# Expert results added onto the kept rows in DRAM by accumulating scatters, in place of a stage that gathers each token's pair of results

## The reference, cut to what matters

```
x = x + gnn(layernorm(x), ...)                       # three attention layers
xf = layernorm(x)
router_logits = einsum('th,eh->te', xf, Wr)
topk_vals, topk_idx = top_k(router_logits, 2)
routing_weights = softmax(topk_vals)
h = gelu(einsum('th,efh->etf', xf, Wi) + bi)
expert_out = einsum('etf,ehf->eth', h, Wo) + bo
out = einsum('tk,tkh->th', routing_weights, the two chosen rows of expert_out)
x = x + out
```

## Time and profile before

| | us |
|---|---|
| median of 3 runs (3463.12 to 3468.98) | 3465.05 |
| the profiled execution | 3468.89 |
| its span, first to last instruction | 3467.1 |
| PE busy | 2769.7 |
| DVE busy | 2306.3 |
| POOL busy | 1486.6 |
| ACT busy | 869.1 |

### The profile page before, as it was taken

The page is one execution under the profiler, slowest core; times in us unless marked ns, Lnnn a source line. Parts: engine busy times, 40 slices in busy tenths (PEclk is TensorE's granted clock), DMA queues, the critical chain, the costliest instruction groups (busy, mean ns, idle before and its releaser), DMA issues.

```text
span 3467.1 us, 58417 instructions
## 1 busy us (share of the span) xinstructions
PE 2769.7 (80%) x14425; PEld 1927.4 (56%) x14426; DVE 2306.3 (67%) x4402; ACT 869.1 (25%) x1640; POOL 1486.6 (43%) x1569
## 2 busy tenths in 40 slices
PE   0797999999889799999979989999994544999910
PEld 0685555555578555555548855555553444677700
DVE  8647999999877699999987746666664444122233
ACT  0221222222244222222234423433431111111100
POOL 1002676767400466676730067777760000211133
PEclk9997999999989899999989989999995555899955
DMA  2334999999744699999964479999976651333366
GB/s 104 100 110 143 312 308 313 312 311 308 239 148 156 214 308 307 311 316 312 307 205 156 150 271 325 331 327 329 329 273 221 221 194 47 110 131 132 123 229 235
DMA packets 225304, 804.36 MB, mean 232 GB/s; under 512 B 35255, under 2 KB 74576, under 8 KB 225252
## 3 DMA queue, kind: packets, MB, share of 16 engines
q0 software_dynamic: 117456, 582.67, 47.6%
q1 hardware_dynamic: 86654, 162.71, 15.9%
q10 hardware_dynamic: 21142, 58.39, 4.3%
HBM read 692.95 MB, written 111.09 MB: 232 GB/s over the span
## 4 chain that ended last, share of the span: by engine, by line
PE 35%; DVE 20%; DMA 17%; POOL 10%; issue 10%; ACT 5%; ACTq 2%; DVEq 1%; SPq 1%; POOLq 0%
PE PS L824 15%; DMA arena<-table,src_k 11%; POOL arena L514 10%; PE PS L932 4%; PE PS L756 4%; PE PS L921 3%; DMA arena<-table 3%; DMA arena<-expert_out,chosen 2%; PE PS L758 2%; DVE parts L1220 2%; DVE arena L1203 2%; PE PS L905 1%; DVE arena L1084 1%; DVE arena L1100 1%; DVE arena L1099 1%
## 5 line engine op out<-in xcount | busy, mean ns | idle before, releaser
L514 POOL DMA_INDIRECT arena<-table,src_k x1260 | 1296.7, 1029 | 522.2 <-PE PS L824 296.5
L824 PE MATMUL PS<-arena,S 128*128 128x396 f32 (+1 forms) x2688 | 992.7, 508 | 9.7 <-DVE arena L1203 9.7
L1203 DVE TENSOR_TENSOR arena<-arena,PS 128x768 f32<-128x768 f32 x840 | 766.1, 944 | 0.9 <-ACT arena L650 0.9
L824 PEld LDWEIGHTS PS<-arena,S 128*128 128x128 f32 x2688 | 470.7, 190 | 240.5 <-issue 28.3
L824 PE MATMUL PS<-parts,S 128*128 128x384 f32 (+2 forms) x1344 | 326.8, 365 | 123.0 <-DVE parts L1220 87.9
L824 PE MATMUL PS<-arena,S_weighted 128*128 128x384 f32 x1008 | 385.2, 511 | 22.6 <-issue 12.5
L801 PEld LDWEIGHTS PS<-erp,ST_b 128*128 128x128 bf16 x3780 | 220.0, 97 | 321.2 <-issue 228.0
L756 PE MATMUL PS<-W_split,S 128*128 128x512 f32 x900 | 358.9, 416 | 27.7 <-DVE xT_rest L1123 27.2
L470 POOL DMA_DIRECT2D table<-arena x75 | 40.7, 543 | 659.9 <-ACT arena L570 635.8
L824 PEld LDWEIGHTS PS<-parts,S 128*128 128x128 f32 x1344 | 220.5, 190 | 138.3 <-issue 137.6
L801 PE MATMUL PS<-erp,ST_b 128*128 x3780 | 254.0, 172 | 14.9 <-DVE ST_b L1169 11.5
(11 more groups left out here) (222 smaller groups left out, 3652.9 us busy)
## 6 DMA issues: line engine op xcount, KB each, us to landing
local_b<-local SPq DMA_DIRECT2D x252, 160.0 KB, 5.6
mixed<-sums ACTq DMA_DIRECT2D x75, 384.0 KB, 6.4
arena<-mixed SPq DMA_DIRECT2D x75, 384.0 KB, 3.8
arena<-table SPq DMA_DIRECT2D x75, 384.0 KB, 5.1
expert_out<-arena SPq DMA_DIRECT2D x56, 384.0 KB, 2.4
arena<-table,src_k POOLq DMA_INDIRECT x1260, 5.3
table<-arena POOLq DMA_DIRECT2D x50, 390.0 KB, 3.4
arena<-in_x SPq DMA_DIRECT2D x48, 384.0 KB, 4.1
```

What stands on the lines that cost most here:

```text
L514: nc.gpsimd.indirect_dma_start(edge_rows(l)[:, k % U, 0:D + HEADS[l]], None, table[l][:, :], bass.IndirectOffsetOnAxis(src_k[:, k:k + 1].b ...
L824: o = nc.tensor.matmul(flat[:, bass.ds(odd * 1024 + 512 * c, n)], onehot, row[:, c * HALF:c * HALF + n], start=False, stop=True, skip_grou ...
L1203: nc.vector.tensor_tensor(z, z, a, ALU.mult).then_inc(s_msg, 1)
```

## The change

Each expert result is multiplied by its gate when DVE copies it out of PSUM, and POOL adds it with an indirect accumulating DMA straight onto the token's row of `x2_kept`. When all 56 slots are added, SP and ACT copy `x2_kept` to the output, from DRAM to DRAM, in two large pieces and one small one. The pair stage, `expert_out`, `chosen` and the two gather helpers of the pair stage are gone.

For this, the gate of each place and slot is found as the token is: two more products of one-hots and gates (`at_gate`) on DVE and 50 more matmuls on PE. Places without a token (gate 0) are aimed at 128 spare rows behind the kept ones, which SP fills with zeros at the start. Two adds may touch the same token, so POOL waits for the landing of add n-1 before it issues add n.

POOL's stages are no longer in a loop: they are written out, with the gather of slot n+2 ahead of the add of slot n. `token_of` is indexed directly.

```
+            sp.wait_ge(s_const, 6)
+            sp.dma_start(x2_kept[NPAD:NPAD + P, :], zeros[:, 0:D]).then_inc(s_spare, 16)
...
+            for q in range(2):
+                sp.wait_ge(s_added[q], 16 * (NS // 2))
+            sp.dma_start(out_rows(0, 8), kept_rows(0, 8)).then_inc(s_out_sp, 16)
+            sp.dma_start(out[N // COPY * COPY:N, :], x2_kept[N // COPY * COPY:N, :]).then_inc(s_out_sp, 16)
+            sp.wait_ge(s_out_sp, 32)
...
+            def gather_tokens(n):
+                if n >= 2:
+                    pool.wait_ge(s_xgTp, n - 1)
+                nc.gpsimd.indirect_dma_start(in0(n % 2), None, normed[:, :], bass.IndirectOffsetOnAxis(
+                    token_of[:, n:n + 1].bitcast(U32), 0)).then_inc(s_xg[n % 2], 16)
+
+            def add_to_tokens(n):
+                pool.wait_ge(s_y, n + 3)
+                if n:
+                    pool.wait_ge(s_added[(n + 1) % 2], 16 * ((n + 1) // 2))
                 pool.sem_inc(s_tick)
+                nc.gpsimd.indirect_dma_start(x2_kept[:, :], bass.IndirectOffsetOnAxis(
+                    target_of[:, n:n + 1].bitcast(U32), 0), zr(n % 2, D), None, compute_op=ALU.add).then_inc(s_added[n % 2], 16)
...
             pool.wait_ge(s_routed, 1)
-            sweep_nodes(pool, [(gather_tokens, 0)], count=NS)
-            for q in range(2):
-                pool.wait_ge(s_y_st[q], 16 * (NS // 2 + 1))
-            sweep_nodes(pool, [(gather_pairs, 0)])
+            for n in range(2):
+                gather_tokens(n)
+            pool.wait_ge(s_spare, 16)
+            pool.wait_ge(s_gates, 1)
+            for n in range(NS):
+                if n + 2 < NS:
+                    gather_tokens(n + 2)
+                add_to_tokens(n)
...
+            act.dma_start(out_rows(8, 15), kept_rows(8, 15)).then_inc(s_out_act, 16)
+            act.wait_ge(s_out_act, 16)
...
             o.then_inc(s_tokens_p, 1)
+            pe.wait_ge(s_gated, 2)
+            for m in range(NB * TOP):
+                o = nc.tensor.matmul(PS[:, 7, 0:NS], at_place()[:, m, :], at_gate(m % TOP)[:, m // TOP, :],
+                                     start=(m == 0), stop=(m == NB * TOP - 1))
+            o.then_inc(s_gates_p, 1)
             pe.wait_ge(s_routed, 1)
+            pe.wait_ge(s_gates, 1)
...
+            for j, g in enumerate((g0, g1)):
+                link(tt(at_gate(j), at_slot().rearrange("p (b j) s -> p b j s", j=TOP)[:, :, j, :],
+                   g.unsqueeze(2).broadcast_to([P, NB, NS]), ALU.mult))
+            dve.sem_inc(s_gated, 2)
...
+            row, spare = routing("row"), routing("spare")
+            nc.vector.tensor_copy(token_of[:, :], PS[:, 6, 0:NS]).then_inc(s_routed, 1)
+            link(ts(spare, zeros[:, 0:NS], own[:, 0:1], float(NPAD), ALU.add, ALU.add))
+            link(tt(row, PS[:, 6, 0:NS], spare, ALU.subtract))
+            dve.wait_ge(s_gates_p, 1)
             for q in range(2):
                 link(nc.vector.memset(hT(q)[FH:FH + 1, :], 1.0))
-            nc.vector.tensor_copy(token_of[:, :], PS[:, 6, 0:NS]).then_inc(s_routed, 1)
+            link(nc.vector.tensor_copy(gate_of[:, :], PS[:, 7, 0:NS]))
+            link(nc.vector.scalar_tensor_tensor(out=row, in0=gate_of[:, :], scalar=0.0, in1=row, op0=ALU.is_gt, op1=ALU.mult))
+            tt(target_of[:, :], row, spare, ALU.add).then_inc(s_gates, 1)
+            dve.wait_ge(s_gates, 1)
 
             def copy_y(b):
                 dve.wait_ge(s_down, b.n + 1)
-                dve.wait_ge(s_y_st[b.q], 16 * b.turn + 16)
-                nc.vector.tensor_copy(zr(b.q, D).rearrange("p (c d) -> p c d", c=2),
-                                      PS[:, 4 + 2 * b.q:6 + 2 * b.q, 0:HALF]).then_inc(s_y, 1)
+                if b.reuse:
+                    dve.wait_ge(s_added[b.q], 16 * b.turn)
+                nc.vector.tensor_scalar(zr(b.q, D).rearrange("p (c d) -> p c d", c=2),
+                                        PS[:, 4 + 2 * b.q:6 + 2 * b.q, 0:HALF], gate_of[:, bass.ds(b.n, 1)], None,
+                                        ALU.mult).then_inc(s_y, 1)
...
-            sweep_nodes(dve, [(result, 0)], dc, 2)
```

More of the change, by code:

```diff
@@ L41 @@
 NS = (TOP * N + EX * (P - 1)) // P
+COPY = 13
 NO_NODE = -1.0
@@ L101, in gnn_ffn @@
         normed = nc.dram_tensor("normed", (NPAD, D), F32, kind="Internal").ap()
-        x2_kept = nc.dram_tensor("x2_kept", (NPAD, D), F32, kind="Internal").ap()
-        expert_out = nc.dram_tensor("expert_out", (NS * P, D), F32, kind="Internal").ap()
+        x2_kept = nc.dram_tensor("x2_kept", (NPAD + P, D), F32, kind="Internal").ap()
         local = nc.dram_tensor("local", (V, P), BF16, kind="Internal").ap()
@@ L130, in gnn_ffn @@
         token_of = sb("token_of", [P, NS], I32)
+        target_of = sb("target_of", [P, NS], I32)
+        gate_of = sb("gate_of", [P, NS])
         place_of = sb("place_of", [P, NB, TOP], I32)
         expert_at = sb("expert_at", [1, NS // 2, 4], I32)
-        chosen = sb("chosen", [P, 4], I32)
         ident = sb("ident", [P, P])
@@ L201, in gnn_ffn @@
         s_onehots = sem("s_onehots"); s_tokens_p = sem("s_tokens_p"); s_routed = sem("s_routed")
-        s_xg = [sem("s_xg0"), sem("s_xg1")]; s_chosen = sem("s_chosen"); s_xgTp = sem("s_xgTp"); s_xgT = sem("s_xgT")
+        s_xg = [sem("s_xg0"), sem("s_xg1")]; s_xgTp = sem("s_xgTp"); s_xgT = sem("s_xgT")
         s_up = sem("s_up"); s_gelu = sem("s_gelu"); s_hTp = sem("s_hTp"); s_hT = sem("s_hT"); s_down = sem("s_down")
-        s_y = sem("s_y"); s_y_st = [sem("s_y_st0"), sem("s_y_st1")]
-        s_ab = [sem("s_ab0"), sem("s_ab1")]; s_x2in = [sem("s_x2in0"), sem("s_x2in1")]; s_or = sem("s_or")
-        s_or_st = [sem("s_or_st0"), sem("s_or_st1")]
+        s_y = sem("s_y"); s_added = [sem("s_added0"), sem("s_added1")]
+        s_spare = sem("s_spare"); s_gated = sem("s_gated"); s_gates_p = sem("s_gates_p"); s_gates = sem("s_gates")
+        s_out_sp = sem("s_out_sp"); s_out_act = sem("s_out_act")
         s_dve = sem("s_dve"); s_acts = sem("s_acts"); s_pool = sem("s_pool"); s_den = sem("s_den"); s_tick_act = sem("s_tick_act"); s_tick_dve = sem("s_tick_dve")
@@ L303, in gnn_ffn @@
         sizes = dict.fromkeys(("lg", "pairs", "t", "one0", "one1", "upto", "other"), NB * EX)
-        sizes |= dict.fromkeys(("best", "v0", "v1", "d", "e", "g0", "g1", "token", "real"), NB)
-        sizes |= dict.fromkeys(("place", "slot"), NB * TOP)
+        sizes |= dict.fromkeys(("best", "v0", "v1", "d", "e", "token", "real"), NB)
+        sizes |= dict.fromkeys(("place", "slot", "gates"), NB * TOP)
         sizes |= dict.fromkeys(("rising", "slots", "last_slot", "swap", "slots_i"), EX)
-        sizes["expert"] = NS
+        sizes |= dict.fromkeys(("expert", "row", "spare"), NS)
         def routing(name):
@@ L317, in at_place, with at_gate @@
         def at_place():
-            return arena[:, 0:NB * TOP * P].rearrange("p (m n) -> p m n", n=P)
+            return arena[:, 2 * D:2 * D + NB * TOP * P].rearrange("p (m n) -> p m n", n=P)
         def at_slot():
-            return arena[:, NB * TOP * P:NB * TOP * (P + NS)].rearrange("p (m n) -> p m n", n=NS)
+            return arena[:, 2 * D + NB * TOP * P:2 * D + NB * TOP * (P + NS)].rearrange("p (m n) -> p m n", n=NS)
+        def at_gate(j):
+            base = ST[:, :, :, :].rearrange("p a b c -> p (a b c)") if j else W_rest[:, F + sum(sizes.values()):]
+            return base[:, 0:NB * NS].rearrange("p (m n) -> p m n", n=NS)
         def ended_at():
-            return arena[0:1, NB * TOP * (P + NS):NB * TOP * (P + NS) + NS * EX].rearrange("o (s e) -> o s e", e=EX)
+            return arena[0:1, 2 * D + NB * TOP * (P + NS):2 * D + NB * TOP * (P + NS) + NS * EX].rearrange("o (s e) -> o s e", e=EX)
         def xT_lead(q):
@@ L342, in erm_flat, with out_rows, kept_rows @@
             return erm[:, :, :].rearrange("p b h -> p (b h)")[:, 0:NB * 2 * HEADS[l]]
+        def out_rows(a, z):
+            at = slice(a * 16 * COPY, min(z * 16, N // COPY) * COPY)
+            return out[at, :].rearrange("(a r) d -> a (r d)", r=COPY)
+        def kept_rows(a, z):
+            at = slice(a * 16 * COPY, min(z * 16, N // COPY) * COPY)
+            return x2_kept[at, :].rearrange("(a r) d -> a (r d)", r=COPY)
         block = ctx.enter_context(nc.Block())
@@ L356, in _ @@
             sp.dma_start(edges[ET - 1:ET, P:P + NE - full], dst[full:NE].rearrange("(t e) -> t e", t=1)).then_inc(s_pad, 16)
-            sp.wait_ge(s_const, 3)
+            sp.wait_ge(s_const, 6)
+            sp.dma_start(x2_kept[NPAD:NPAD + P, :], zeros[:, 0:D]).then_inc(s_spare, 16)
             pad = P - (NE - full)
@@ L477, in keep_rows @@
                 nc.gpsimd.dma_start(normed[bass.ds(b.row0(), P), :], xr(b.q)).then_inc(s_kept[b.q], 16)
-            def gather_tokens(b):
-                if b.reuse:
-                    pool.wait_ge(s_xgTp, b.n - 1)
-                pool.sem_inc(s_tick)
[L484 to L502, removed]
+            def gather_tokens(n):
[7 more added lines that the diff above has]
```

(18 more changed lines are left out.)

## The result

The changed kernel takes 3844.01 us (median of 4, 3841.26 to 3846.87) against 3467.02 us of the kernel before in the same comparison: ratio 1.1088, 95% interval 1.1069 to 1.1107. It is 377 us slower. The forecast was 3674 with a range to 3825. So the direction and the loop that it named came out, but the size was 170 us short, 19 us beyond the range.

The account below looks back on a forecast made before the run. PE alone was taken to pace the expert tiles before, a one-tile wait loop after the change. 3468.89 + 313.2 (loop) + 19.7 (routing) - 123.9 (end) - 3.84 (profile to median) gave 3674 us, range 3560 to 3825.

Parts of the forecast that it names:

- The closed loop: Expert tiles: gather(m) can't be issued before down(m-3) is done, which closes a loop of one tile; +313 us.
- its signs: Expert stage: PE idle 4 to 5 us per tile, POOL awaiting DVE's scaled copy, gather issued 1.3 us after add.
- The routing: Before the tiles: DVE products 3.1, fifty more matmuls 21.6, small operations 1.5, less the old wait 6.5; +19.7 us.
- The end: After the last result's copy: last add, then a 9.6 MB DRAM copy, 39.5 us instead of 163.4; -123.9 us.
- The sum of the loop: Expert tiles: 10.83 us per tile at full clock, 14.3 at the low one, taken as 12.0 against 6.09.
- Wake of POOL: In the expert loop, from the end of the awaited step to POOL's start: 0.25 us.
- Issue of the add and gap: In the expert loop on POOL, from the add's start to the gather's start: 1.28 us.
- The gather's landing: In the expert loop, gather issue to PE's wake: 4.73 us behind another indirect DMA, 3.95 alone; 4.73 taken.
- PE's part: In the expert loop, turn and down: 3.46 us at full clock, 6.9 at the low, a third of tiles low.
- The scaled copy: In the expert loop, DVE's copy with gate: 0.96 us, gate priced at nothing, bound +0.06 (1.02).
- rival 2: Expert tiles, slow adds: an add lands after 10.2 us, the gather behind only then; 16.4 per tile, 3906 us; chance 0.14.
- Rival 3: Expert tiles: gathers stay hidden, PE keeps 6.09 us; 3361 us; faster if the tile is below 8.06; chance 0.04.

Follow-up runs that it names:

- the run on the kernel before: Kernel before, one wait added on POOL: the gather of slot n waits for DVE's copy of the result of slot n-3; 3782.94 us, ratio 1.0910.

## Why the prediction was wrong in size and right in kind

**The closed loop: right.** PE idle before its turn, POOL waiting for the scaled copy, the gather behind the add, two speeds of PE's work: as foretold in kind. The figures of its signs were off with the sum: PE stands idle 6.5 us per tile and not 4 to 5, the gather starts 1.9 after the add and not 1.3, and the up matmuls (line 921 before, 926 now) take 4.20 in the first two tiles only and 2.11 or 2.12 in the other 54. The order alone costs 315 us (the run on the kernel before), and undoing it takes back 454 us.

**The routing: right.** +19.9 for +19.7; the gate matmuls ran at the low clock throughout.

**The end: right.** -119.5 for -123.9. The last landing of the two large copies came 31.9 us after its issue, for 29.0 + 3.1. The missing 4 us are in front of it: the last three adds stand in a row, each waiting for the one before, 6.1 to 7.0 us apart, while PE's last two tiles run faster than that. I had priced one add there, not the chain.

**The sum of the loop: this step failed.** It was 12.0 and measured 15.1, and 53 tiles make 164 us of that. By its terms:

- *Wake of POOL, 0.25, measured 0.86 (0.91 in the mean).* I took the wake of a POOL copy. The row for a DMA behind a wait and an increment stood right under it, 0.81, and I had even quoted it as part of what falls away. The run without the increment takes 0.58 of it away: +0.65.
- *Issue of the add and gap, 1.28, measured 1.90.* An accumulating indirect DMA is issued in 1.59 and not 0.97. Nothing in the trace of before showed it, and I bounded its landing from both sides but not its issue: +0.6.
- *The gather's landing, 4.73, measured 5.2.* Above both of my values (3.95 and 4.73): +0.5. That it depends on the add ahead of it was right, but not for the reason I had. Being behind another DMA costs nothing by itself (3.9 behind a plain scatter); being behind an accumulating one costs 1.2 us. So the 4.73 of the second gather of the earlier trace rows probably has another reason: loads and other gathers ran beside it. No run tests that. The Trainium skill (Collectives: The Full Stack, "The bandwidth ceiling: the fold count and why AG ≠ RS ≠ AR") has the reducing step of a ring collective at half the rate of the copying one, because its add reads two sources. The prediction carried this over to a kernel's own accumulating DMA, as an estimate of 1.2 us. For the gather queued behind the add the trace agrees (5.1 against 3.9); for the add's own landing it doesn't (5.6 against 3.0, 2.6 us more). That the second read is the cause is not shown by any run here.
- *PE's part, 4.6 (3.46 at the high clock, 6.9 at the low, a third of the tiles at the low), measured 5.8 in the mean.* Both ends were right, and that the clock would move between them; the mixture was wrong in kind. The clock doesn't change from tile to tile but within each: up, right after the down, runs at the high clock (2.11 us) in all but the first two tiles; the turn, right after the idle stretch, runs at the low one (1.54), and so does most of the down (4.5 in the mean, between 2.75 and 5.5). The mean over the stretch, 0.72, says that 44% of the time has the high clock, but little of that is the part in the loop: +1.2.
- *The scaled copy, 0.96, takes 1.02*, the bound that I had named; with the wait before it (0.24 for 0.15) +0.15.

These make 3.1 us. That is against the 12.0, which had some clock loss and some delay of the gather in it. By the runs the clock's whole share is 2.4 us per tile, the accumulation's 1.5 (1.8 direct, 0.4 given back by PE's part), the increment's 1.0 (0.58 direct).

**The range.** Its upper end took PE at the low clock throughout, 14.3, but left issue and wake at single values. The wake at the 0.81 of the earlier trace rows alone would have put it at about 3855, above what was measured; with the issue at 1.59 too, which no row of before showed, the dearest loop would have been 15.5 and the end about 3890. Of the rivals, none came: rival 2 put the loss on a landing of 10.2 us for the add and it was 5.6. Rival 3 named the right place: with the gather a slot further ahead the tile falls below its point of 8.06 and the kernel is faster than before.

## What to carry to other kernels

When a step moves onto an in-order queue that also feeds the pipeline, write down for each item what must have happened for the item in front of it. If one of these is the consumer's own last step, a loop of one tile is closed, here in spite of two buffers. In this kernel one line's place decides between 11% slower and 2.3% faster. Price every term of such a loop by a row of the same kind of instruction with the same kind of wait, and take for the engine whose clock changes the speed that it has just after its idle stretch, not its mean.

## What the runs showed that I had not expected

- A semaphore increment written between a wait and a DMA on POOL costs 0.58 us when an engine's signal ends the wait, and nothing measurable when a landing ends it (0.85 us from the landing to the next add, with it and without). It costs nothing either where nothing is left to wait for: in the run with the gather ahead of the add, the add with its increment starts 0.30 us after the gather's issue ends, as a gather without one does. Why it is hidden in these two cases stays open.
- An accumulating scatter delays the gather queued behind it by 1.2 us, though its own landing is 2.6 us longer than a plain one's (5.6 and 3.0). It is also issued 0.6 us slower.
- Work added to an engine that waits made the kernel 115 us faster, since it kept the clock up.
- A copy of 9.6 MB from DRAM to DRAM in two large pieces took 31.9 us, some 300 GB/s by the bytes moved once, near the 331 that the reads of the layers reach: no sign that reading and writing add up.
